# The router gate folded into a shared expert's first weights, and routing one iteration later, in a mixture-of-experts kernel

## What is computed

```python
mod = (silu(c) @ wmod).reshape(1, 6, 1, 512)       # sa, ca, ga, sb, cb, gb
h = layernorm(x) * (1 + ca) + sa
x = x + ga * (tanh(h @ B.T) @ C.T + D * h)
h = layernorm(x) * (1 + cb) + sb
scores = sigmoid(h @ gate_w.T)                      # 2048 x 8
idx = top_k(scores + router_bias, 2)
w = scores[idx] / sum(scores[idx])
y_e = (silu(h @ W1[e]) * (h @ W3[e])) @ W2[e]       # 512 -> 352 -> 512
shared = (silu(h @ sw1.T) * (h @ sw3.T)) @ sw2.T    # 512 -> 704 -> 512
x = x + gb * (sum_e w_e * y_e + shared)
```

## Time and profile before

| | |
|---|---|
| time, median of 3 runs | 629.92 us (628.85 to 631.08) |
| the profiled execution | 630.82 us, its span 628.90 us |
| TensorE busy | 568.8 us, 90% of the span |
| VectorE busy | 334.4 us, 53% |
| GpSimd busy | 241.0 us, 38% |
| ScalarE busy | 177.8 us, 28% |
| granted clock of TensorE, mean | 0.97 |

### The profile page before, as it was taken

How to read it: one execution, slowest core, us unless ns; L and a number is a source line. 1 busy time by engine, 2 the same in 40 slices (tenths; PEclk the granted TensorE clock), 3 DMA queues, 4 the chain that set the end, 5 groups by cost and what they waited for, 6 DMA issues and landing times.

```text
span 628.9 us, 11739 instructions
## 1 busy us (share of the span) xinstructions
PE 568.8 (90%) x3304; PEld 509.3 (81%) x3305; DVE 334.4 (53%) x710; ACT 177.8 (28%) x331; POOL 241.0 (38%) x199
## 2 busy tenths in 40 slices
PE   5767889999999977599998999989999999999995
PEld 2445779889889767489997999979999999999994
DVE  1577879789788768532221232222223224766766
ACT  1230533433433331123222232223223222122120
POOL 1386738547547625151017500073461003232231
PEclk9977989999999998799999999999999999999998
DMA  8970556213313323675246752269662224445443
GB/s 316 352 261 1 201 198 243 98 59 113 110 43 117 109 102 130 203 304 209 83 130 217 296 220 82 73 208 347 228 225 70 97 67 151 152 156 168 145 134 117
DMA packets 37560, 102.72 MB, mean 163 GB/s; under 512 B 4256, under 2 KB 4256, under 8 KB 36640
## 3 DMA queue, kind: packets, MB, share of 16 engines
q1 hardware_dynamic: 27952, 53.65, 24.9%
q0 software_dynamic: 9152, 47.98, 21.4%
q10 hardware_dynamic: 432, 0.79, 0.3%
HBM read 71.73 MB, written 30.67 MB: 163 GB/s over the span
## 4 chain that ended last, share of the span: by engine, by line
PE 66%; DVE 15%; issue 7%; POOL 5%; DMA 3%; ACT 1%; SPq 1%; DVEq 0%; POOLq 0%
PE bank L767 11%; PE bank L769 11%; PE bank L768 11%; PE bank L781 6%; PE bank L783 6%; PE bank L782 6%; PE bank L753 4%; PE bank L788 3%; DVE ra L1027 2%; PE bank L729 2%; POOL wlo L460 2%; DVE sel L1020 2%; DMA whi<-w_all 1%; PE bank L839 1%; PE bank L718 1%
## 5 line engine op out<-in xcount | busy, mean ns | idle before, releaser
L767 PE MATMUL bank<-whi,thi 128*128 x416 | 139.5, 335 | 5.3 <-POOL wlo L460 3.4
L768 PE MATMUL bank<-wlo,thi 128*128 x416 | 135.1, 325 | 0.0
L769 PE MATMUL bank<-whi,tlo 128*128 x416 | 134.9, 324 | 0.0
L781 PE MATMUL bank<-whi,gth 128*128 (+1 forms) x204 | 81.8, 401 | 4.5 <-DVE wlo L1126 2.0
L767 PEld LDWEIGHTS bank<-whi,thi 128*128 128x128 f32 x416 | 78.8, 189 | 6.5 <-issue 6.5
L460 POOL TENSOR_TENSOR wlo<-raw,whi 128x1408 f32 (+3 forms) x21 | 68.9, 3304 | 37.7 <-DMA whi<-w_all 37.6
L1360 DVE TENSOR_TENSOR gbuf<-s,bank 128x352 f32<-128x352 f32 x52 | 27.0, 519 | 104.1 <-ACT s L697 103.9
L782 PE MATMUL bank<-wlo,gth 128*128 (+1 forms) x204 | 81.1, 397 | 0.0
L783 PE MATMUL bank<-whi,gtl 128*128 (+1 forms) x204 | 80.9, 397 | 0.0
L1364 DVE TENSOR_TENSOR gtl<-bank,gth 128x384 fp32r<-128x384 f32 x52 | 29.0, 558 | 97.6 <-ACT gth L701 91.8
L768 PEld LDWEIGHTS bank<-wlo,thi 128*128 128x128 f32 x416 | 79.1, 190 | 0.0
(11 more groups left out here) (183 smaller groups left out, 1067.5 us busy)
## 6 DMA issues: line engine op xcount, KB each, us to landing
raw<-w_all POOLq DMA_DIRECT2D x7, 2176.0 KB
whi<-w_all POOLq DMA_DIRECT2D x14, 704.0 KB
h<-xs_rows SPq DMA_DIRECT2D x36, 256.0 KB
ys_rows<-tmpa SPq DMA_DIRECT2D x36, 256.0 KB, 2.0
whi<-w_all POOLq DMA_DIRECT2D x7, 768.0 KB, 13.2
x_all<-wmod SPq DMA_DIRECT2D x4, 1024.0 KB, 9.3
x_all<-x SPq DMA_DIRECT2D x4, 1024.0 KB, 9.1
hs_rows<-h SPq DMA_DIRECT2D x8, 512.0 KB, 2.8
```

The source lines that it names most:

```text
L767: pe.matmul(dst, xh[:, j, a], wh, start=(m == 0), stop=False)
L768: pe.matmul(dst, xh[:, j, a], wl, start=False, stop=False)
L769: mm = pe.matmul(dst, xl[:, j, a], wh, start=False, stop=(m == KD - 1))
L781: pe.matmul(dst, gth[:, a], wh, start=(m == 0), stop=False)
```

## The change

The gate's eight columns are put in front of W1 in each of shared expert A's four blocks of weights, so that the first half of each block is 360 columns wide: the logits fall out of `up` in columns 0 to 7 of bank 2. ScalarE copies them to lg behind each silu, and takes the sigmoid of both tiles of a pair at the end of its iteration. The gate's own matmuls and the xtf copies stay for the last pair alone. Steps 0 to 19 of a pair, its ranks and its scatter come one iteration later (`it - 4` for `it - 3`), from iteration 4 on; the ranks stand at the end of TensorE's iteration, and steps 13 to 19 in one piece behind gtl of the second tile. In iteration 10 the pairs 6 and 7 are both routed and scattered, 6 first. The weights of expert A are written into their slot with the new stride, and all others shift by SH = 32 columns.

```diff
--- before.py
+++ after.py
@@ -47,6 +47,8 @@
+UPA = UP + E
+SH = KD * E
...
@@ -96,8 +98,8 @@
-        whi = sb("whi", [P, 2 * WSZ], F32R)
-        wlo = sb("wlo", [P, 2 * WSZ], F32R)
+        whi = sb("whi", [P, SH + 2 * WSZ], F32R)
+        wlo = sb("wlo", [P, SH + 2 * WSZ], F32R)
...
+        whi_a, wlo_a = (w[:, 0:KD * UPA].rearrange("p (k c) -> p k c", c=UPA) for w in (whi, wlo))
...
+        def of_slot_a(w, w_a, k):
+
+            a, b = PIECES[k]
+            if k < NW - 1:
+                h = KD // (NW - 1)
+                return w_a[:, h * k:h * k + h, E:UPA], raw[:, a:b].rearrange("p (k c) -> p k c", c=UP)
+            return w[:, SH + a:SH + b], raw[:, a:b]
...
+        def routes(lo, hi):
+
+            return lo - 4 >= 0 and hi - 4 < NP - 1
...
@@ -344,16 +362,19 @@
             def body(it, lo, hi):
-                if live(3, lo, hi):
-                    p = it - 3
+                if routes(lo, hi):
+                    p = it - 4
                     left = value(sp, p * 64)
                     sp.wait_ge(s_nat, p * 16 + 16)
-                    if is_last(lo):
-                        sp.wait_ge(s_xd, NP)
-                    elif lo > 3:
+                    if lo > 4:
                         sp.wait_ge(s_scat, left)
-                    sp.dma_start(hrow[is_last(lo)], hs[bass.ds(p * 2 * P, 2 * P), :].rearrange("(b p) d -> p b d", p=P)
-                                 ).then_inc(s_hrow[is_last(lo)], 16)
+                    sp.dma_start(hrow[0], hs[bass.ds(p * 2 * P, 2 * P), :].rearrange("(b p) d -> p b d", p=P)
+                                 ).then_inc(s_hrow[0], 16)
+                if is_last(lo):
+                    sp.wait_ge(s_nat, NP * 16)
+                    sp.wait_ge(s_xd, NP)
+                    sp.dma_start(hrow[1], hs[(NP - 1) * 2 * P:NP * 2 * P, :].rearrange("(b p) d -> p b d", p=P)
+                                 ).then_inc(s_hrow[1], 16)
...
@@ -500,23 +522,22 @@
-                if live(3, lo, hi) and is_last(lo):
-                    scatter()
-                if live(3, lo, hi) and not is_last(lo):
-                    scatter()
+                if is_last(lo):
+                    scatter(it - 4, 0)
+                    scatter(it - 3, 1)
+                if routes(lo, hi) and not is_last(lo):
+                    scatter(it - 4, 0)
                 if lo in (NP, NP + 1):
                     low(1, WSZ, [[0, 1], [2]][lo - NP])
...
@@ -592,7 +613,10 @@
-                act.activation(s1[:, :], bank[2][:, 0:F], ACT.Silu).then_inc(q["A", "silu"], 1)
+                act.activation(s1[:, :], bank[2][:, E:E + F], ACT.Silu).then_inc(q["A", "silu"], 1)
+                if not is_last(lo):
+                    act.activation(lg[:, bass.ds(p * 2 + j, 1), :].rearrange("p a e -> p (a e)"), bank[2][:, 0:E],
+                                   ACT.Copy).then_inc(s_lg, 1)
...
@@ -623,17 +647,15 @@
                     for j in range(2):
                         act.activation(xah[:, j, :], bank[4 + j][:, :], ACT.Copy).then_inc(q["A", "xhi"], 1)
-                        act.activation(xtf[:, j, :], bank[4 + j][:, :], ACT.Copy).then_inc(s_xtf, 1)
-
-                    act.wait_ge(s_gate, p + 1)
-                    act.activation(sc[:, bass.ds(p * 2, 2), :],
-                                   bank[7][:, 0:2 * E].rearrange("p (b e) -> p b e", b=2),
-                                   ACT.Sigmoid).then_inc(s_sc, 1)
+                        if is_last(lo):
+                            act.activation(xtf[:, j, :], bank[4 + j][:, :], ACT.Copy).then_inc(s_xtf, 1)
+                    if is_last(lo):
+                        act.wait_ge(s_gate, 1)
+                        act.activation(sc[:, bass.ds(p * 2, 2), :],
+                                       bank[7][:, 0:2 * E].rearrange("p (b e) -> p b e", b=2),
+                                       ACT.Sigmoid).then_inc(s_sc, 1)
...
@@ -656,6 +678,11 @@
                 if live(3, lo, hi):
                     hidden(it - 3, 1, lo)
+                    if not is_last(lo):
+                        p = it - 3
+                        act.wait_ge(s_lg, p * 2 + 2)
+                        act.activation(sc[:, bass.ds(p * 2, 2), :], lg[:, bass.ds(p * 2, 2), :],
+                                       ACT.Sigmoid).then_inc(s_sc, 1)
...
@@ -671,6 +698,8 @@
+            act.wait_ge(l_gate, 32)
+            act.activation(whi_a[:, :, 0:E], gw[:, :, :], ACT.Copy).then_inc(s_gwh, 1)
...
@@ -761,9 +790,12 @@
                     for h in range(2):
-                        w = off + (m * UP + h * F)
-                        wh, wl = whi[:, bass.ds(w, F)], wlo[:, bass.ds(w, F)]
-                        dst = bank[2 + h][:, 0:F]
+                        if sec == "A":
+                            w, n = m * UPA + h * (E + F), F + (1 - h) * E
+                        else:
+                            w, n = off + (SH + m * UP + h * F), F
+                        wh, wl = whi[:, bass.ds(w, n)], wlo[:, bass.ds(w, n)]
+                        dst = bank[2 + h][:, 0:n]
...
@@ -861,9 +869,36 @@
                 if is_last(lo):
-                    ranks()
+                    last_tile()
+                    ranks(it - 4)
+                    pe.wait_ge(s_xtf, 2)
+                    pe.wait_ge(s_rt, (it - 4) * KR + 15)
+                    for j in range(2):
+                        for k in range(KD):
+                            mm = pe.matmul(bank[7][:, j * E:(j + 1) * E], xtf[:, j, k * P:(k + 1) * P],
+                                           gw[:, k, :], start=(k == 0), stop=(k == KD - 1))
+                    mm.then_inc(s_gate, 1)
...
@@ -878,9 +913,9 @@
                 if live(3, lo, hi):
+                    if not is_last(lo):
+                        pe.wait_ge(s_lg, (it - 3) * 2 + 1)
                     up("A", it - 3, 1, 0)
-                    if not is_last(lo):
-                        ranks()
...
@@ -1121,15 +1156,14 @@
                 def between(*which):
-                    if not is_last(lo):
-                        route(it, lo, hi, *which)
+                    if routes(lo, hi) and not is_last(lo):
+                        route(it - 4, lo, *which)
...
                 if is_last(lo):
-                    route(it, lo, hi, *range(13))
+                    route(it - 4, lo, *range(KR))
+                    route(it - 3, lo, *range(13))
                 between(0)
...
                 if live(3, lo, hi):
                     product_a(it - 3, 1, lo)
-                between(13, 14, 15)
                 if live(3, lo, hi):
                     finish_a(it - 3, 0, lo)
-                between(16)
                 if live(3, lo, hi):
                     low_a(it - 3, 1, lo)
-                between(17, 18, 19)
+                between(*range(13, KR))
...
@@ -1279,6 +1315,9 @@
             dve.wait_ge(l_gate, 32)
+            dve.wait_ge(s_gwh, 1)
+            dve.tensor_tensor(wlo_a[:, :, 0:E], gw[:, :, :], whi_a[:, :, 0:E].bitcast(F32),
+                              ALU.subtract).then_inc(s_gwl, 1)
```

More of the change, by code:

```diff
@@ L136, in build @@
         sc = sb("sc", [P, NT, E])
+        lg = sb("lg", [P, NT, E])
         oh = [sb("oh1", [P, NT, E]), sb("oh2", [P, NT, E])]
@@ L501, in body, with scatter @@
                     fetch(0, WSZ, lambda: None)
[L503 to L505 removed]
+                def scatter(p, last):
+                    landed, known = 16 if last else value(pool, p * 16 + 16), value(pool, p * KR + KR)
                     pool.wait_ge(s_fold, 1)
[L507 removed]
+                    pool.wait_ge(s_hrow[last], landed)
                     pool.wait_ge(s_rt, known)
@@ L863, in body @@
                 if is_last(lo):
-                    ranks()
-                if live(3, lo, hi):
-                    pe.wait_ge(s_xtf, (it - 3) * 2 + 2)
+                    last_tile()
[7 more added lines that the diff above has]
+                    mm.then_inc(s_gate, 1)
+                if live(3, lo, hi):
+                    if lo == hi == 3:
+                        pe.wait_ge(w_ready, NW - 1)
+                        pe.wait_ge(s_gwl, 1)
+                    if live(1, lo, hi):
+                        pe.wait_ge(s_tlo, (it - 1) * 2 + 2)
+                    if lo > 3:
+                        pe.wait_ge(q["A", "g"], (it - 3) * 2)
+                        pe.wait_ge(s_lg, (it - 3) * 2)
+                    up("A", it - 3, 0, 0)
+                if live(2, lo, hi):
+                    pe.wait_ge(s_x1, (it - 2) * 2 + 2)
+                if live(4, lo, hi) and not is_last(lo):
+                    last_tile()
+                if is_last(lo):
+                    ranks(it - 3)
+                if live(3, lo, hi):
+                    if is_last(lo):
+                        pe.wait_ge(s_xtf, 2)
+                    else:
+                        pe.wait_ge(q["A", "xhi"], (it - 3) * 2 + 2)
                     pe.wait_ge(q["A", "g"], (it - 3) * 2 + 1)
@@ L1003, in finish_a, with route @@
```

(10 more changed lines are left out.)

67 lines of the change are left out of this document (20 added, 47 removed).

## The result

The changed kernel is slower: a median of 637.35 us (635.94 to 638.48, four runs) against 629.88 (628.85 to 631.08, four runs), a ratio of 1.0113, 95% interval 1.0094 to 1.0132. The forecast was 627.4, range 624.0 to 631.0. (Of the executions of a run further down, e2, one took 1139.05 us; the figures there are those of the other three.) Its profiled execution took 638.48 us with a span of 636.8, 7.9 us more than the span before.

The account below looks back on a forecast made before the run. The prediction took GpSimd's serial stretch, 15.04 of the 23.62 us cycle, to bound the loop. Its terms, -2.6 - 1.0 - 0.8 + 1.9 = -2.5 us from the median 629.92, gave 627.4 us, range 624.0 to 631.0.

Parts of the forecast that it names:

- Mask makes it, by half a microsecond: Iteration 10, VectorE: mask of pair 6 starts at +5.15, ahead of the 3.51 us wlo step at +5.66, and passes.
- What bounds the loop: Steady loop: GpSimd's serial stretch, 15.04 of the 23.62 us cycle, sets the pace, not TensorE.
- The first rival: Loop: TensorE is the bound after all, -11 us more, about 616 us; chance 0.12.
- Iterations 3 and 4, -2.6: Before the steady loop: -1.0 in iteration 3, the rest in iteration 4; first idx about 2.6 us earlier.
- the -1.7 for the gate: Iteration 4, TensorE sets the pace: removing the gate's matmuls saves 1.7 us.
- Steady iterations, -1.0: Iterations 5 to 8: cycle 23.37 us against 23.62, 0.25 us won in each of four, -1.0 us.
- The stretch of 15.04 us: Loop, GpSimd from idx's end through scatters, D*x and deviations: keeps its length; the prediction falls if it changes.
- Table switch, 0: ScalarE between gth and thi: the moved sigmoid and table load delay thi about 1 us, with room, costing nothing.
- the second rival: ScalarE between gth and thi: dear table switch delays sel, +0.85 us an iteration, +4.6 in all, 634.5 us; chance 0.10.
- Iteration 9, -0.8: Iteration 9: sel gets in before GpSimd's 6.39 us wlo step; gain 1.0 us if so, 0.3 if not, taken -0.8.
- Iteration 10, +1.9: Last iteration: routing pairs 6 and 7 there costs +1.0 us for the mask and +0.9 for low-clock TensorE, +1.9.
- the third rival: Iteration 10: mask of pair 6 falls behind the wlo step, +3.9 us instead of +1.9, 629.4 us; chance 0.2.

Follow-up runs that it names:

- e2: Kernel before, the first expert's three wlo steps on GpSimd cut to 16 columns each (output not the reference's): 624.65 us, ratio 0.9914.
- e4: Changed kernel without the fold: logits again from 16 gate matmuls per pair on xtf, sigmoid at its old place, routing still late: 637.87 us, ratio 1.0109.
- e5: Changed kernel, GpSimd's second D*x add done for the first tile of a pair only (output not the reference's): 630.18 us, ratio 1.0001.
- e6: Kernel before, GpSimd's second D*x add done for the first tile of a pair only (output not the reference's): 624.65 us, ratio 0.9914.
- e1: Changed kernel, the first expert's three wlo steps on GpSimd cut to 16 columns each (output not the reference's): 628.05 us, ratio 0.9971.
- e9: Changed kernel, full work, the first expert's three wlo steps moved from GpSimd to VectorE behind the tables: 629.37 us, ratio 0.9985.
- e8: Kernel before, full work, the first expert's three wlo steps moved from GpSimd to VectorE behind the tables: 625.65 us, ratio 0.9928.
- e10: e9 with the gate matmuls of pair 7 ahead of the rank matmuls of pair 6 in the last iteration: 626.50 us, ratio 0.9928.
- e7: e10 plus e3's edit and separate buffers for pair 6's positions and rows: 620.43 us, ratio 0.9848.
- e3: Changed kernel, pair 6's 13 routing steps up to mask placed ahead of the two xal steps in the last iteration: 631.41 us, ratio 1.0024.
- e12: e2 with 512 columns in the third wlo step (output not the reference's): 624.55 us in a single execution.

## Why the prediction was wrong

The step that failed is the last iteration's: forecast +1.9 us, measured +7.84. Its sentence "Mask makes it, by half a microsecond" let mask of pair 6 pass ahead of the wlo step; it was held for 4.03 us instead, and two pairs' routing in series behind it cost more than the forecast gave it. A second step failed by less: iteration 9, forecast -0.8, measured +0.98. Term by term:

- **What bounds the loop:** right, and shown by e4, e5 and e6. The first rival (TensorE) is out: e4 puts the gate back on TensorE, and no mark moves by more than 0.53 us.
- **Iterations 3 and 4, -2.6:** -2.63, first idx at 112.38, and both parts as reckoned (-1.02 and -1.61). But the -1.7 for the gate is not what made it: e4 keeps the gate and has its first idx at 111.86. There the gate costs 1.3 us in iteration 4, and its absence in the changed kernel went with the longer idle time and the low clock in iteration 3. That the sum came out to 0.03 is in part luck.
- **Steady iterations, -1.0:** -0.13. The stretch of 15.04 us, on which "all of the loop is hung", became 15.23 to 15.38. What follows it came out as reckoned: 23.56 - 15.23 = 8.33 us, where the forecast had 23.37 - 15.04 = 8.33 and before had 8.58. The longer stretch took that gain back. It is the change that the prediction named as the one that would make it fall.
- **Table switch, 0:** right; the second rival did not occur. The drain of about 1.38 us that the Trainium skill states (page "ScalarE: Activation LUTs", section "What ACT_TABLE_LOAD costs") doesn't show here either: the load starts 0.02 us after gth ends, and the sigmoid 0.01 us after the load.
- **Iteration 9, -0.8:** +0.98, off by 1.8. "Gets in before it" failed: sel came at +5.68 rather than +5.4, level with the wlo step. At +5.4 it would most likely have fared no better, by the steps that were held from 0.53 to 0.59 us ahead. And my lower bound, 0.3 of gain if sel missed, was no bound. sel now came first to be held, for both steps, with gbuf behind it; TensorE went idle and slow. e1 and e9 show what the hold hid: without it the iteration takes 17.8 us against 20.0 in e2 and e8, so here the change does pay, 2.2 us.
- **Iteration 10, +1.9:** +7.84, the step that decided. "Mask makes it, by half a microsecond" took a recorded start for the start of the hold, although the row that I had read and put there, sel at 235.96 with 4.13 us, starts 0.58 us before the wlo step and is held. Mask's place was right, +5.11 for +5.15: it was not late, as the third rival had it, and was held all the same. For the rest that rival was what happened, and its place for mask of pair 7, +14.7 to +16.4, is close to the +16.57 found. After that both were mis-sized: gbuf, which stands before the rank steps, waited for the silu of an up product that began only behind the gate and at the low clock, so from mask to idx it was 5.32 us instead of 2.34. The forecast had taken 0.9 of these 3.0 us (at most 1.4), the rival none. Its chance of 0.2 was too low, since the row spoke for it.
- Even with no hold at all, in e9, this iteration takes 19.24 us against 11.76 in e8: two pairs' routing in series, each with a wait of TensorE in it, costs 7.5 us, more than the 5.25 us by which e9 is ahead of e8 when it begins. I had given 1.9 for it. e10 and e7 recover most of it by order and buffers alone.
- **The experts, 0:** they took 1.9 us more in the profiled execution. The 10 us over the second change of weights show a clock of 0.83 there, and 1.00 in the kernel before. e3 and e6 show the same dip and e1, e2, e4 and e5 don't, so it goes with neither kernel. It is not the whole of the 1.9: e4 and e9, without the dip, took 367.9 us for the experts. Where the rest arises stays open.

## What to carry to other kernels

Count what a software pipeline's last iteration does when a stage is moved one iteration later: two stages meet there with no steady work to hide them, and their order on each engine is a choice to be made anew. Where a long step on one engine holds another, it costs whatever stands in that other's queue; such steps can go to a place where that engine waits anyway, or on that engine itself (e8 and e9). Freeing an engine that is 95% busy in the loop was worth nothing while a serial stretch elsewhere set the cycle; it was worth something after that stretch was cut.

## What the hardware did that I had not expected

- The hold begins before the GpSimd step's recorded start. Behind a scatter, steps of VectorE that started 0.53 to 0.59 us ahead of it were held to its end, in five executions (before, changed, e4, e5, e6) with 1536 columns and in e12 with 512; steps that ended 0.57 or more ahead were not. With 16 columns (e1, e2) a step 0.55 to 0.58 us ahead took its usual 0.17 to 0.19. Why the short one doesn't hold stays open. The Trainium skill, page "Perfetto Trace Analysis", section "GPSIMD Engine Instruction", says that such an instruction's start is reported when it issues the read of its operands, after it has begun to execute. If the hold began with the execution, it would begin where these rows have it; no run shows that it does.
- A step of VectorE with one input is held too: idx, a TENSOR_SCALAR from float32 to uint32, for 1.71 us in e3. The Trainium skill, page "SBUF — State Buffer", section "Who interferes with whom", names tensor_scalar among the operations that can take the shared pair of ports, when their operands meet certain conditions.
